# Linear-attention stage of a two-layer transformer: its loop over 128 units written out one to three units ahead

## The chip, the cores and the metric

One Trainium2 chip with 8 NeuronCores. All 8 cores run the same program, each on one sequence of 2048 tokens by 1024 features; they exchange nothing. The metric is the device time of the slowest core in microseconds (us), as the median of the timed runs.

## The reference, cut to what matters

The network has two pre-norm layers: ordinary attention and a ternary-weight feed-forward part in the first, linear attention and a gated feed-forward part in the second. The change touches only the linear attention of the second layer:

```python
def taylor_exp(x):                       # x: (b, h, l, 16) -> (b, h, l, 1 + 16 + 256)
    x2 = (x[..., :, None] * x[..., None, :]).reshape(*x.shape[:-1], d * d) / r2
    return jnp.concatenate([ones, x / rrd, x2 / rd], axis=-1)
q = (hidden @ Wq) ; k = (hidden @ Wk) ; v = (hidden @ Wv)     # 16 heads, q and k 16 wide, v 64 wide
qf, kf = taylor_exp(q), taylor_exp(k)
A = jnp.tril(jnp.einsum('bhnf,bhmf->bhnm', qf, kf))
y = jnp.einsum('bhnm,bhme->bhne', A, v)
z = 1.0 / (jnp.einsum('bhlf,bhlf->bhl', qf, jnp.cumsum(kf, axis=2)) + EPS)
out = (y * z[..., None]) ... @ Wo
```

## The kernel before

The program is a row of stages (`p0` to `p11`, all inside `build_program`). In each stage every engine has its own list of instructions, collected by a helper class `Ph` (its `op`, `wait` and `dma` record instructions, which is why nearly all of them carry line 52 in the profile, and waits line 84), and the stages are separated by a barrier. Engines are kept in step by hand: `ts` counts what TensorE has finished, `vs` what VectorE has, `ss` what ScalarE has, and `p.wait(engine, semaphore, value)` puts a wait into that engine's list. The order of each engine's work is exactly the order in which the Python code records it.

The changed stage is `p7` (from line 870 on). It computes the linear attention in chunks of 256 tokens. Its inputs lie in SBUF: `QF` and `KF` (projections with the feature on the partitions), `QTK` and `KTK` (the same with the token on the partitions, scaled) and `V1` (values, with a column of ones per head, so that the denominator is computed as a 65th output). A unit is one head and one chunk: `units` (line 905) has 16 heads by 8 chunks, 128 in all, with two heads (`lane` 0 and 1) alternating, so that unit `ui` and unit `ui - 2` belong to the same head and the state is carried from one to the other.

For each unit (loop at line 962) the code records, in this order:

1. VectorE: `RHQ` (the head's 16 rows of `QF`, by a mask), then the key features in `KFB`, per half chunk a product of 16 by 16 and a scaled copy, then a drain (lines 965 to 981).
2. ScalarE, from the second chunk on: the running state `PST` copied to `STSB` (lines 983 to 986).
3. TensorE: the score products `PG` (lines 988 to 998).
4. ScalarE: `ARAW`, the square of the shifted scores, since the second-order expansion of the exponential is a square plus 0.5 (line 1002).
5. VectorE: `ASB`, plus 0.5 and the triangular mask, three instructions (lines 1005 to 1012).
6. TensorE: `PY`, two products with the values, and from the second chunk on three with the state and the transposed query features `QFM`; then six products that add to the state `PST` (lines 1014 to 1045).
7. ScalarE: the reciprocal of the denominator as Ln, drain, Exp (`ZSC`, `Z`).
8. TensorE: `Z` broadcast over 64 partitions by a product with ones, written over `PG` (line 1054).
9. VectorE: `PY` copied to `YT`, a drain, and the product with the broadcast into `Y` (lines 1058 to 1067).
10. `prep_qf(ui + 2)` (line 950), if that unit isn't of chunk 0: VectorE builds the query features in `QFTK`, TensorE transposes them in two times three blocks to `PTR`, two tensors of 384 columns, and VectorE copies each to `QFM` (lines 927 to 942).

There are two buffers each of `KFB`, `QFTK`, `QFM`, `RHQ`, `ARAW`, `ASB`, `STSB`, `Z`, `YT`, and of the PSUM tensors `PST`, `PG`, `PY` and `PTR`, eight banks in all. The one transfer of the stage, the weights `WO1` of the next, is issued at its start.

Of the kernel before, what the change touches and what calls it, by code (L numbers as in the profile page):

```python
# [20 lines left out]
S1 = 1.0 / math.sqrt(4.0 * math.sqrt(2.0))  # L21
# [125 lines left out]
def build_program(T=2048, upto="p11", taps=()):  # L147
# [14 lines left out]
    nc = bass.Bass("TRN2", target_bir_lowering=False)  # L162
# [40 lines left out]
    dst = [Sem(st, nc, f"dst{i}") for i in range(2)]  # L203
# [7 lines left out]
    ts = Sem(st, nc, "ts")  # L211
# [128 lines left out]
    p = Ph()  # L340
# [529 lines left out]
    if act("p7"):  # L870
# [3 lines left out]
        with ExitStack() as ps:  # L874
            KFB = [ps.enter_context(nc.sbuf_tensor(f"KFB{i}", [128, 2 * 384], BF16)) for i in range(2)]
            QFTK = [ps.enter_context(nc.sbuf_tensor(f"QFTK{i}", [128, 2 * 384], BF16)) for i in range(2)]
            QFM = [ps.enter_context(nc.sbuf_tensor(f"QFM{i}", [128, 3 * 256], BF16)) for i in range(2)]
            RHQ = [ps.enter_context(nc.sbuf_tensor(f"RHQ{i}", [128, 256], BF16)) for i in range(2)]
# [8 lines left out]
            PY = [ps.enter_context(nc.psum_tensor(f"PY{i}", [65, 256], F32)) for i in range(2)]  # L887
            PTR = [ps.enter_context(nc.psum_tensor(f"PTR{i}", [128, 384], BF16)) for i in range(2)]
            zb_ts = {}

            p = Ph()
            p.dma("gpsimd", WO1[:, :], dram["wo1"], dq1)
            for b in KFB:
                p.add("vector", lambda v, b=b: v.memset(
                    b.rearrange("p (s f) -> p s f", s=2)[:, :, 0:1], 1.0))
                p.add("vector", lambda v, b=b: v.memset(
                    b.rearrange("p (s f) -> p s f", s=2)[:, :, 273:384], 0.0))
            for b in QFTK:
# [62 lines left out]

            for ui, (h, ch) in enumerate(units):
                lane = h // 8
                kc = lane
                p.wait("vector", ts, g_ts.get(ui - 2, 0))
                p.op("vector", "tensor_single_scalar", RHQ[lane][:, :],
                     QF[:, kc * T + ch * 256: kc * T + ch * 256 + 256],
                     HMASK[:, (h % 8):(h % 8) + 1], AL.mult)
                p.wait("vector", ts, state_ts.get(ui - 2, 0))
                for tsub in range(2):  # L970
                    tt = 2 * ch + tsub
                    src = KTK[:, tt * 256 + h * 16: tt * 256 + h * 16 + 16]
                    i0 = src.unsqueeze(1).broadcast_to([128, 16, 16])
                    i1 = src.unsqueeze(2).broadcast_to([128, 16, 16])
                    p.op("vector", "tensor_tensor",
                         KFB[lane][:, tsub * 384 + 17: tsub * 384 + 273].rearrange(
                             "p (i j) -> p i j", i=16), i0, i1, AL.mult)
                    p.op("vector", "tensor_scalar_mul",
                         KFB[lane][:, tsub * 384 + 1: tsub * 384 + 17], src, 0.5 / S1)
                p.op("vector", "drain", inc=vs)  # L980
                stage_vs = vs.n
                if ch > 0:
                    p.wait("scalar", ts, state_ts.get(ui - 2, 0))
                    p.wait("scalar", ts, y_ts.get(ui - 2, 0))
                    p.op("scalar", "activation", STSB[lane][:, :], PST[lane][:, :],
                         AF.Copy, inc=ss)
                    evac_ss[ui] = ss.n
                p.wait("tensor", vs, stage_vs)
                if ch > 0:
                    p.wait("tensor", ss, evac_ss[ui])  # L990
                p.wait("tensor", ss, araw_ss.get(ui - 2, 0))
                p.wait("tensor", vs, yv_vs.get(ui - 2, 0))
                p.op("tensor", "matmul", PG[lane][:, 0:256],
                     KF[:, kc * T + (2 * ch) * 128: kc * T + (2 * ch) * 128 + 128],
                     RHQ[lane][:, :], start=True, stop=True)
                p.op("tensor", "matmul", PG[lane][:, 256:384],
                     KF[:, kc * T + (2 * ch + 1) * 128: kc * T + (2 * ch + 1) * 128 + 128],
                     RHQ[lane][:, 128:256], start=True, stop=True, inc=ts)
                g_ts[ui] = ts.n
                p.wait("scalar", ts, g_ts[ui])  # L1000
                p.wait("scalar", vs, a_vs.get(ui - 2, 0))
                p.op("scalar", "activation", ARAW[lane][:, 0:384], PG[lane][:, 0:384],
                     AF.Square, scale=1.0 / math.sqrt(32.0), bias=CB[:, 2:3], inc=ss)
                araw_ss[ui] = ss.n
                p.wait("vector", ss, araw_ss[ui])
                p.wait("vector", ts, y_ts.get(ui - 2, 0))
                p.op("vector", "scalar_tensor_tensor", ASB[lane][:, 0:128],
# [4 lines left out]
                     ARAW[lane][:, 256:384], 0.5, TRIL[:, :], AL.add, AL.mult, inc=vs)  # L1012
                a_vs[ui] = vs.n
                p.wait("tensor", vs, a_vs[ui])
                p.wait("tensor", vs, yv_vs.get(ui - 2, 0))
                mms = [
# [17 lines left out]
                y_ts[ui] = ts.n  # L1034
                for tsub in range(2):
                    first = (ch == 0 and tsub == 0)
                    for fcx in range(3):
                        p.op("tensor", "matmul",
                             PST[lane][:, fcx * 65: fcx * 65 + 65],
                             KFB[lane][:, tsub * 384 + fcx * 128: tsub * 384 + fcx * 128 + 128],  # L1040
                             V1[:, (2 * ch + tsub) * 1040 + h * 65: (2 * ch + tsub) * 1040 + h * 65 + 65],
                             start=(first and fcx == 0), stop=(tsub == 1 and fcx == 2),
                             skip_group_check=True,
                             inc=(ts if (tsub == 1 and fcx == 2) else None))
                state_ts[ui] = ts.n
                p.wait("scalar", ts, y_ts[ui])
                p.wait("scalar", ts, zb_ts.get(ui - 2, 0))
# [4 lines left out]
                z1_ss = ss.n  # L1052
                p.wait("tensor", ss, z1_ss)
                p.op("tensor", "matmul", PG[lane][0:64, 0:256], ONES_B[64:65, 0:64],
                     Z1[lane][64:65, :], start=True, stop=True, skip_group_check=True,
                     inc=ts)
                zb_ts[ui] = ts.n
                p.wait("vector", ts, y_ts[ui])
                p.wait("vector", ss, z1_ss)
                p.wait("vector", vs, yv_vs.get(ui - 2, 0))  # L1060
# [4 lines left out]
                p.op("vector", "tensor_mul",
                     Y[64 * (h % 2): 64 * (h % 2) + 64,
                       (h // 2) * T + ch * 256: (h // 2) * T + ch * 256 + 256],
                     YT1[lane][:, :], PG[lane][0:64, 0:256], inc=vs)
                yv_vs[ui] = vs.n
                if ui + 2 < len(units):  # L1070
                    prep_qf(ui + 2)
            p.emit(nc)
# [174 lines left out]
```

How the kernel before makes its waits and increments, by code:

```python
        def f(e, meth=meth, a=a, kw=kw, tgt=tgt, inck=inck, lowp=lowp):  # L47
            if lowp:
                with e.bass.allow_low_precision("bf16 output by design"):
                    ins = getattr(e, meth)(*a, **kw)
            else:
                ins = getattr(e, meth)(*a, **kw)
            if tgt is not None:
                ins.then_inc(tgt, inck)
# [6 lines left out]
        def f(e, o=out_ap, i=in_ap, h=sem.h):  # L61
            e.dma_start(o, i).then_inc(h, 16)
# [6 lines left out]
        def f(e, o=out_ap, i=in_ap, h=sem.h):  # L69
            e.dma_start_transpose(o, i).then_inc(h, 16)
# [8 lines left out]
        def f(e, h=sem.h, v=v):  # L79
            e.wait_ge(h, v)
```

## Time and profile before

| | us |
|---|---|
| median of the timed runs | 4940.17 (4936.41 to 4943.93) |
| the profiled execution, whole | 4869.27 |
| its span, first to last instruction, slowest core | 4867.7 |
| spans of the 8 cores | 4851.3 to 4867.7 |
| granted TensorE clock, mean over the span, 1 is 2.4 GHz | 0.728 |

The table is to be read so: the timed runs have no profiler, and the profiled execution is a single one; durations of instructions come from it. Its time beside its span shows how little lies outside the recorded instructions.

### The profile page before, as it was taken

The numbers are of one execution on the slowest core, as the hardware profiler recorded it, in microseconds if no ns is written. First come the engines' busy times: TensorE is split into PE (matmuls) and PEld (weight loads), VectorE is DVE, ScalarE is ACT, GpSimd is POOL, SyncE is SP. The second block draws the span as 40 slices with busy tenths as digits, with TensorE's granted clock in tenths as the row PEclk, the third lists the DMA queues.
The fourth block names the chain that finished last, engine by engine and source line by source line (L and its number), as shares of the span: only waits on it lengthen the run. The fifth ranks groups of instructions, "written<-read, shape, count | busy, mean of one in ns | idle before, by whom it ended". The sixth has DMA issues, their size and how long they took to land. (4 is left out here: it accounts for less than half of the span.)

```text
span 4867.7 us, 39062 instructions; the slowest of 8 cores (4851.3 to 4867.7 us)
## 1 busy us (share of the span) xinstructions
PE 2552.6 (52%) x12011; PEld 1046.0 (21%) x12136; DVE 1620.0 (33%) x3557; ACT 1177.4 (24%) x1691; POOL 109.6 (2%) x162
## 2 busy tenths in 40 slices
PE   1556556456456500039996563333333336378877
PEld 0221111111112200014442331111111112133333
DVE  2332432432432464540002234444444443422221
ACT  1345245245245200023121211111111113211110
POOL 0000000000000001100000000000000000000000
PEclk8778678678678755569998775555555557699999
DMA  4000000000000075612321100000000000335525
GB/s 99 7 1 7 7 1 7 7 1 7 0 1 1 29 261 192 203 39 78 71 59 35 26 18 1 1 1 1 1 1 1 1 1 1 48 52 73 63 39 108
DMA packets 178933, 188.15 MB, mean 39 GB/s; under 512 B 118432, under 2 KB 159408, under 8 KB 175024
## 3 DMA queue, kind: packets, MB, share of 16 engines
q0 software_dynamic: 90400, 126.92, 12.5%
q1 hardware_dynamic: 88336, 58.72, 4.3%
q8 instruction: 108, 1.77, 0.2%
q14 instruction: 89, 0.73, 0.1%
HBM read 211.85 MB, written 25.17 MB: 49 GB/s over the span
## 5 line engine op out<-in xcount | busy, mean ns | idle before, releaser
L52 ACT ACTIVATE SCR<-S,NEGC 128x1024 bf16<-128x1024 f32 x512 | 548.2, 1112 | 151.5 <-PE S L52 147.7
L52 PE MATMUL PO<-SCR,VP 128*65 128x512 bf16 x1024 | 346.4, 423 | 168.5 <-ACT SCR L52 93.0
L52 DVE CAST Y<-PO 64x512 bf16<-64x512 f32 x64 | 43.7, 684 | 630.2 <-PE PO L52 629.7
L52 PE MATMUL PGU<-XLN,WGS 128*128 128x512 bf16 x752 | 181.1, 380 | 120.1 <-DVE HH L52 94.4
L52 DVE TENSOR_TENSOR X<-X,TF 128x512 f32<-128x512 f32 x64 | 44.3, 693 | 582.5 <-ACT TF L52 582.5
L52 PE MATMUL lnA<-lnXB,ONES_B 128*1 128x512 bf16 x128 | 56.9, 624 | 343.5 <-ACT lnXB L52 343.5
L52 ACT ACTIVATE ARAW<-PG,CB 128x384 bf16<-128x384 f32 x128 | 74.4, 581 | 665.3 <-PE PG L52 665.2
L52 PE MATMUL PH<-XLN,W1S 128*128 128x512 bf16 x1003 | 222.0, 381 | 17.2 <-DMA W1S<-w1b 15.1
L52 PE MATMUL PH<-HSB,W2S 128*128 128x512 bf16 x1004 | 220.3, 379 | 2.9 <-ACT HSB L52 1.9
L52 PE MATMUL S<-QP,KP 64*128 64x512 bf16 x1024 | 216.4, 430 | 5.1 <-DVE NEGC L52 5.1
L50 DVE RECIPROCAL DROW<-DROW 1x512 bf16<-1x512 bf16 x64 | 206.6, 3292 | 0.8
L52 PE MATMUL PG<-RHQ,KF 128*128 128x256 bf16 (+1 forms) x256 | 61.1, 341 | 269.4 <-DVEq L52 269.4
L52 PE MATMUL PTR<-IDN,QFTK 128*128 128x128 bf16 x672 | 89.5, 304 | 202.9 <-DVE QFTK L52 202.9
L52 PE MATMUL PAUX<-DROW,ONES_B 1*64 1x512 bf16 x64 | 38.4, 600 | 284.7 <-DVE DROW L50 232.4
L52 PE MATMUL PY<-ASB,V 128*65 128x256 bf16 (+1 forms) x256 | 64.1, 353 | 226.3 <-DVE ASB L52 226.3
L52 PE MATMUL PGU<-XLN,WUS 128*128 128x512 bf16 x753 | 180.6, 380 | 0.8
L52 ACT ACT_TABLE_LOAD x11 | 14.1, 1283 | 635.3 <-PEq L84 441.7
L52 PE MATMUL PGU<-HH,WDS 128*128 128x512 bf16 x752 | 165.4, 379 | 2.9 <-DVE HH L52 2.0
L52 DVE CAST YT<-PY 64x256 bf16<-64x256 f32 x128 | 53.4, 417 | 334.8 <-ACT Z L52 334.8
L52 DVE TENSOR_TENSOR TT<-SGT,PGU 128x512 bf16<-128x512 bf16 x96 | 66.0, 687 | 296.1 <-ACT SGT L52 296.1
L52 DVE SCALAR_TENSOR_TENSOR ASB<-ARAW,TRIL 128x128 bf16<-128x128 bf16 x256 | 73.8, 288 | 241.6 <-ACT ARAW L52 241.5
L52 ACT ACTIVATE SGT<-PGU 128x512 bf16<-128x512 f32 x96 | 57.3, 597 | 377.7 <-PE PGU L52 377.7
(157 smaller groups left out, 3708.8 us busy)
## 6 DMA issues: line engine op xcount, KB each, us to landing
WSL<-w POOLq DMA_DIRECT2D x16, 2048.0 KB, 11.8
WSL<-w POOLq DMA_DIRECT2D x64, 512.0 KB, 4.2
W1S<-w1b SPq DMA_DIRECT2D x16, 1024.0 KB, 5.4
W2S<-w2b SPq DMA_DIRECT2D x16, 1024.0 KB, 6.6
WGS<-wg POOLq DMA_DIRECT2D x12, 1024.0 KB, 9.2
WUS<-wu POOLq DMA_DIRECT2D x12, 1024.0 KB, 13.5
WDS<-wd POOLq DMA_DIRECT2D x16, 768.0 KB, 8.1
w1b<-WTB SPq DMA_DIRECT2D x8, 1024.0 KB, 5.0
```

Of the source, the lines that this page charges most:

```text
L50: ins = getattr(e, meth)(*a, **kw)
L52: ins = getattr(e, meth)(*a, **kw)
```

## The change

The loop body is cut into small functions, each recording one step of unit `i` on one engine, and a new loop calls them for different units. Buffers follow: `KFB` gets two per lane, `QFM` three, the two `PTR` become one of 768 columns, and the broadcast of `Z` gets a bank of its own, `PZB`, of which there is one.

```diff
-            KFB = [ps.enter_context(nc.sbuf_tensor(f"KFB{i}", [128, 2 * 384], BF16)) for i in range(2)]
+            KFB = [[ps.enter_context(nc.sbuf_tensor(f"KFB{i}_{j}", [128, 2 * 384], BF16))
+                    for j in range(2)] for i in range(2)]
-            QFM = [... for i in range(2)]
+            QFM = [... for i in range(3)]
-            PTR = [ps.enter_context(nc.psum_tensor(f"PTR{i}", [128, 384], BF16)) for i in range(2)]
+            PTR = ps.enter_context(nc.psum_tensor("PTR", [128, 768], BF16))
+            PZB = ps.enter_context(nc.psum_tensor("PZB7", [64, 256], F32))
...
+            def v_build(i):          # RHQ and KFB
+                p.wait("vector", ts, g_ts.get(i - 2, 0))
...
+                p.wait("vector", ts, state_ts.get(i - 4, 0))
...
+                p.op("vector", "drain", inc=vs)
+            def v_qft(i):            # QFTK
+                p.wait("vector", ts, tr_ts.get(i - 2, 0))
...
+            def t_tr(i):
+                p.wait("tensor", vs, qft_vs[i])
+                p.wait("tensor", vs, ptr_evac_vs.get(i - 2, 0))
...
+            def v_qfm_evac(i):
+                p.wait("vector", ts, tr_ts[i])
+                p.wait("vector", ts, y_ts.get(i - 3, 0))
+                src = PTR.rearrange("p (t c f) -> p t c f", t=2, c=3)
+                dst = QFM[i % 3].rearrange("p (c t f) -> p t c f", c=3, t=2)
+                p.op("vector", "tensor_copy", dst, src, inc=vs)
...
+            def t_g_state(i):        # PG, then the six products into PST
+                p.wait("tensor", vs, build_vs[i])
                 if ch > 0:
+                    p.wait("tensor", ss, evac_ss[i])
+                p.wait("tensor", ss, araw_ss.get(i - 2, 0))
...
+            def t_zb(i):
+                p.wait("tensor", ss, z_ss[i])
+                p.wait("tensor", vs, yv_vs.get(i - 1, 0))
+                p.op("tensor", "matmul", PZB[:, :], ONES_B[64:65, 0:64],
+                     Z1[lane][64:65, :], start=True, stop=True, inc=ts)
...
+            def v_yout(i):           # YT, drain, Y
...
+                p.wait("vector", ts, zb_ts[i])
+                p.op("vector", "tensor_mul", ..., YT1[lane][:, :], PZB[0:64, :], inc=vs)
...
+            v_build(0)
+            for j in (1, 2):
+                if j < NU:
+                    v_qft(j)
+
+            for i in range(NU):
+                t_g_state(i)
+                if i >= 1:
+                    t_zb(i - 1)
+                if i + 2 < NU:
+                    t_tr(i + 2)
+                if i + 1 < NU:
+                    s_evac(i + 1)
+                s_square(i)
+                v_poly(i)
+                if i + 2 < NU:
+                    v_qfm_evac(i + 2)
+                if i + 1 < NU:
+                    v_build(i + 1)
+                if i + 3 < NU:
+                    v_qft(i + 3)
+                t_y(i)
+                s_z(i)
+                if i >= 1:
+                    v_yout(i - 1)
+            t_zb(NU - 1)
+            v_yout(NU - 1)
```

TensorE's list for one unit in the middle of the stage, before the change; a name in brackets is the semaphore waited on (`vs` VectorE's, `ss` ScalarE's):

```order
L52 MATMUL PG<-RHQ,KF 128x256 [waits vs,ss]
L52 MATMUL PG<-RHQ,KF 128x128
L52 MATMUL PY<-ASB,V 65x256 [waits vs]
L52 MATMUL PY<-ASB,V 65x128
L52 MATMUL PY<-QFM,STSB 65x256 x3
L52 MATMUL PST<-V,KFB 128x65 x6
L52 MATMUL PG<-Z_1,ONES_B 64x256 [waits ss]
L52 MATMUL PTR<-IDN,QFTK 128x128 [waits vs]
L52 MATMUL PTR<-IDN,QFTK 128x128 x2
L52 MATMUL PTR<-IDN,QFTK 128x128 [waits vs]
L52 MATMUL PTR<-IDN,QFTK 128x128 x2
```

And the same place in the changed kernel:

```order
L52 MATMUL PG<-RHQ,KF 128x256 [waits vs,ss]
L52 MATMUL PG<-RHQ,KF 128x128
L52 MATMUL PST<-V,KFB_0 128x65 x6
L52 MATMUL PZB<-Z_1,ONES_B 64x256 [waits ss,vs]
L52 MATMUL PTR<-IDN,QFTK 128x128 [waits vs]
L52 MATMUL PTR<-IDN,QFTK 128x128 x5
L52 MATMUL PY<-ASB,V 65x256 [waits vs]
L52 MATMUL PY<-ASB,V 65x128
L52 MATMUL PY<-QFM,STSB 65x256 x3
```

The products into `PST` moved ahead of `PY`; the broadcast of `Z` (now that of the unit before) and the transposes (now of two units later) moved between them and `PY`, and the broadcast waits on VectorE too.

VectorE's list for one unit before the change, from the masks on:

```order
L52 SCALAR_TENSOR_TENSOR ASB<-ARAW,TRIL 128x128 [waits ss,ts]
L52 TENSOR_SCALAR ASB<-ARAW 128x128
L52 SCALAR_TENSOR_TENSOR ASB<-ARAW,TRIL 128x128
L52 CAST YT_1<-PY 64x256 [waits ts,ss,vs]
L52 TENSOR_TENSOR Y<-YT_1,PG 64x256 [waits ts]
L52 TENSOR_TENSOR QFTK<-QTK 128x256
...
L52 COPY QFM<-PTR 128x3x128 [waits ts] x2
L52 TENSOR_SCALAR RHQ<-QF,HMASK 128x256 [waits ts]
L52 TENSOR_TENSOR KFB<-KTK 128x256 [waits ts]
```

And in the changed kernel:

```order
L52 SCALAR_TENSOR_TENSOR ASB<-ARAW,TRIL 128x128 [waits ss,ts]
L52 TENSOR_SCALAR ASB<-ARAW 128x128
L52 SCALAR_TENSOR_TENSOR ASB<-ARAW,TRIL 128x128
L52 COPY QFM<-PTR 128x2x3x128 [waits ts]
L52 TENSOR_SCALAR RHQ<-QF,HMASK 128x256 [waits ts]
L52 TENSOR_TENSOR KFB_1<-KTK 128x256 [waits ts]
...
L52 TENSOR_TENSOR QFTK<-QTK 128x256 [waits ts]
...
L52 CAST YT_0<-PY 64x256 [waits ts,ss,vs]
L52 TENSOR_TENSOR Y<-YT_0,PZB 64x256 [waits ts]
```

`YT` and `Y` (of the unit before) moved from behind the masks to the end of the iteration, and one copy with a destination of one more dimension stands directly behind the masks.

## Rows read from the trace of the kernel before

**Rows 1.** The page's slices, 40 equal parts of the span, in tenths.

```profile
PE   1556556456456500039996563333333336378877
...
PEclk8778678678678755569998775555555557699999
```

**Rows 2.** Windows: length, busy PE, PEld, DVE, ACT, POOL, clock, DMA; timeline: last instruction.

```profile
2859.50:4059.00 1199.50, 406.71 (x2418) 213.06 (x2420) 490.56 (x1960) 214.05 (x497) 0.54 (x1) 0.50 0.01 2
...
4057.00 0.41 DVE L52 TENSOR_TENSOR Y<-YT,PG 64x256 bf16<-64x256 bf16 x1 [0.19 <-PE PG L52]
```

**Rows 3.** Waits in 2860 to 4058 us: waiter, releaser, total us, times, longest.

```profile
ACT ARAW L52 <- PE PG L52: 665.2, 127, 5.9
...
DVE YT L52 <- ACT Z L52: 334.8, 128, 3.0
...
PE PG L52 <- DVEq L52: 269.4, 128, 3.6
```

**Rows 4.** Timeline of one unit: start, duration, engine, instructions, idle before and releaser.

```profile
3397.09 0.48 PE L52 MATMUL PG<-RHQ,KF 128*128 128x256 bf16 x2 [2.05 <-DVEq L52]
3397.72 0.58 ACT L52 ACTIVATE ARAW<-PG,CB 128x384 bf16<-128x384 f32 x1 [5.60 <-PE PG L52]
3398.47 0.29 DVE L52 SCALAR_TENSOR_TENSOR ASB<-ARAW,TRIL 128x128 bf16<-128x128 bf16 x1 [1.88 <-ACT ARAW L52]
...
3398.78 0.28 DVE L52 SCALAR_TENSOR_TENSOR ASB<-ARAW,TRIL 128x128 bf16<-128x128 bf16 x1
...
3399.32 0.50 PE L52 MATMUL PY<-ASB,V 128*65 128x256 bf16 x2 [1.75 <-DVE ASB L52]
...
3400.75 0.38 ACT L52 ACTIVATE ZSC<-PY 1x256 f32<-1x256 f32 x1 [2.45 <-PE PY L52]
3401.19 0.41 ACT L52 ACTIVATE Z<-ZSC 1x256 bf16<-1x256 f32 x1
3401.62 0.34 ACT L52 ACTIVATE STSB<-PST 128x195 bf16<-128x195 f32 x1
...
3401.74 0.39 PE L52 MATMUL PG<-Z,ONES_B 1*64 1x256 bf16 x1 [0.71 <-ACT Z L52]
3401.77 0.42 DVE L52 CAST YT<-PY 64x256 bf16<-64x256 f32 x1 [2.71 <-ACT Z L52]
3402.38 0.41 DVE L52 TENSOR_TENSOR Y<-YT,PG 64x256 bf16<-64x256 bf16 x1 [0.19 <-PE PG L52]
3402.82 0.43 DVE L52 TENSOR_TENSOR QFTK<-QTK 128x256 bf16<-128x256 bf16 x1
...
3403.57 0.17 DVE L52 TENSOR_SCALAR QFTK<-QTK 128x16 bf16<-128x16 bf16 x1
...
3404.01 0.80 PE L52 MATMUL PTR<-IDN,QFTK 128*128 128x128 bf16 x6 [1.87 <-DVE QFTK L52]
3404.66 0.68 DVE L52 COPY QFM<-PTR 128x384 bf16<-128x384 bf16 x2 [0.91 <-PE PTR L52]
3405.25 0.28 DVE L52 TENSOR_SCALAR RHQ<-QF,HMASK 128x256 bf16<-128x256 bf16 x1
3405.45 0.42 DVE L52 TENSOR_TENSOR KFB<-KTK 128x256 bf16<-128x256 bf16 x1
...
3406.19 0.17 DVE L52 TENSOR_SCALAR KFB<-KTK 128x16 bf16<-128x16 bf16 x1
...
3406.86 0.48 PE L52 MATMUL PG<-RHQ,KF 128*128 128x256 bf16 x2 [2.05 <-DVEq L52]
```

**Rows 5.** The same unit by windows, columns as in rows 2.

```profile
3397.09:3406.86 9.77, 3.39 (x21) 1.77 (x22) 4.05 (x16) 1.70 (x4) 0.00 (x0) 0.50 0.00 0
```

**Rows 6.** Groups by line and form on VectorE, copies out of PSUM: count, busy us, mean ns.

```profile
L52 DVE COPY QFM<-PTR 128x384 bf16<-128x384 bf16 x224 | 75.9, 358 | 103.8 <-PE PTR L52 102.9 <-issue 1.0
L52 DVE CAST YT<-PY 64x256 bf16<-64x256 f32 x128 | 53.4, 417 | 334.8 <-ACT Z L52 334.8
...
L52 DVE CAST Y<-PO 64x512 bf16<-64x512 f32 x64 | 43.7, 684 | 630.2 <-PE PO L52 629.7
```

More of the change, by code:

```diff
@@ L874, in build_program @@
         with ExitStack() as ps:
-            KFB = [ps.enter_context(nc.sbuf_tensor(f"KFB{i}", [128, 2 * 384], BF16)) for i in range(2)]
+            KFB = [[ps.enter_context(nc.sbuf_tensor(f"KFB{i}_{j}", [128, 2 * 384], BF16))
+                    for j in range(2)] for i in range(2)]
             QFTK = [ps.enter_context(nc.sbuf_tensor(f"QFTK{i}", [128, 2 * 384], BF16)) for i in range(2)]
-            QFM = [ps.enter_context(nc.sbuf_tensor(f"QFM{i}", [128, 3 * 256], BF16)) for i in range(2)]
+            QFM = [ps.enter_context(nc.sbuf_tensor(f"QFM{i}", [128, 3 * 256], BF16)) for i in range(3)]
             RHQ = [ps.enter_context(nc.sbuf_tensor(f"RHQ{i}", [128, 256], BF16)) for i in range(2)]
@@ L887, in build_program @@
             PY = [ps.enter_context(nc.psum_tensor(f"PY{i}", [65, 256], F32)) for i in range(2)]
-            PTR = [ps.enter_context(nc.psum_tensor(f"PTR{i}", [128, 384], BF16)) for i in range(2)]
-            zb_ts = {}
+            PTR = ps.enter_context(nc.psum_tensor("PTR", [128, 768], BF16))
+            PZB = ps.enter_context(nc.psum_tensor("PZB7", [64, 256], F32))
             p = Ph()
             p.dma("gpsimd", WO1[:, :], dram["wo1"], dq1)
[L893 to L897, printed above, removed]
+            for bb in KFB:
+                for b in bb:
+                    p.add("vector", lambda v, b=b: v.memset(
+                        b.rearrange("p (s f) -> p s f", s=2)[:, :, 0:1], 1.0))
+                    p.add("vector", lambda v, b=b: v.memset(
+                        b.rearrange("p (s f) -> p s f", s=2)[:, :, 273:384], 0.0))
             for b in QFTK:
@@ L960, in build_program, with U @@
                 prep_qf(1)
-            for ui, (h, ch) in enumerate(units):
+            def U(i):
+                return units[i]
+            def v_build(i):
+                h, ch = U(i)
                 lane = h // 8
-                kc = lane
-                p.wait("vector", ts, g_ts.get(ui - 2, 0))
+                kb = (i // 2) % 2
+                p.wait("vector", ts, g_ts.get(i - 2, 0))
                 p.op("vector", "tensor_single_scalar", RHQ[lane][:, :],
-                     QF[:, kc * T + ch * 256: kc * T + ch * 256 + 256],
+                     QF[:, lane * T + ch * 256: lane * T + ch * 256 + 256],
                      HMASK[:, (h % 8):(h % 8) + 1], AL.mult)
-                p.wait("vector", ts, state_ts.get(ui - 2, 0))
+                p.wait("vector", ts, state_ts.get(i - 4, 0))
                 for tsub in range(2):
@@ L980, in build_program @@
                 p.op("vector", "drain", inc=vs)
-                stage_vs = vs.n
-                if ch > 0:
[L983 to L990, printed above, removed]
@@ L991, in build_program @@
-                p.wait("tensor", ss, araw_ss.get(ui - 2, 0))
-                p.wait("tensor", vs, yv_vs.get(ui - 2, 0))
+                build_vs[i] = vs.n
+            def v_qft(i):
+                h, ch = U(i)
+                if ch == 0:
+                    return
+                buf = i % 2
+                p.wait("vector", ts, tr_ts.get(i - 2, 0))
+                for tsub in range(2):
+                    tt = 2 * ch + tsub
+                    src = QTK[:, tt * 256 + h * 16: tt * 256 + h * 16 + 16]
+                    i0 = src.unsqueeze(1).broadcast_to([128, 16, 16])
+                    i1 = src.unsqueeze(2).broadcast_to([128, 16, 16])
+                    p.op("vector", "tensor_tensor",
+                         QFTK[buf][:, tsub * 384 + 17: tsub * 384 + 273].rearrange(
+                             "p (i j) -> p i j", i=16), i0, i1, AL.mult)
+                    p.op("vector", "tensor_scalar_mul",
+                         QFTK[buf][:, tsub * 384 + 1: tsub * 384 + 17], src, 0.5 / S1,
+                         inc=(vs if tsub == 1 else None))
+                qft_vs[i] = vs.n
@@ new lines, in t_tr @@
+            def t_tr(i):
+                h, ch = U(i)
+                if ch == 0:
+                    tr_ts[i] = ts.n
+                    return
+                p.wait("tensor", vs, qft_vs[i])
+                p.wait("tensor", vs, ptr_evac_vs.get(i - 2, 0))
+                for tsub in range(2):
+                    for fcx in range(3):
+                        p.op("tensor", "transpose",
+                             PTR[:, tsub * 384 + fcx * 128: tsub * 384 + fcx * 128 + 128],
+                             QFTK[i % 2][:, tsub * 384 + fcx * 128: tsub * 384 + fcx * 128 + 128],
+                             IDN[:, :],
+                             inc=(ts if (tsub, fcx) == (1, 2) else None))
+                tr_ts[i] = ts.n
@@ new lines, in v_qfm_evac, with s_evac @@
+            def v_qfm_evac(i):
+                h, ch = U(i)
+                if ch == 0:
+                    return
+                p.wait("vector", ts, tr_ts[i])
[3 more added lines that the diff above has]
+                p.op("vector", "tensor_copy", dst, src, inc=vs)
+                ptr_evac_vs[i] = vs.n
+            def s_evac(i):
+                h, ch = U(i)
+                lane = h // 8
+                if ch == 0:
+                    return
+                p.wait("scalar", ts, state_ts.get(i - 2, 0))
+                p.wait("scalar", ts, y_ts.get(i - 2, 0))
+                p.op("scalar", "activation", STSB[lane][:, :], PST[lane][:, :],
+                     AF.Copy, inc=ss)
+                evac_ss[i] = ss.n
@@ new lines, in t_g_state @@
+                for tsub in range(2):
+                    first = (ch == 0 and tsub == 0)
+                    for fcx in range(3):
+                        p.op("tensor", "matmul",
+                             PST[lane][:, fcx * 65: fcx * 65 + 65],
+                             KFB[lane][kb][:, tsub * 384 + fcx * 128: tsub * 384 + fcx * 128 + 128],
+                             V1[:, (2 * ch + tsub) * 1040 + h * 65: (2 * ch + tsub) * 1040 + h * 65 + 65],
+                             start=(first and fcx == 0), stop=(tsub == 1 and fcx == 2),
+                             skip_group_check=True,
+                             inc=(ts if (tsub == 1 and fcx == 2) else None))
@@ L1002, in build_program, with s_square @@
+                state_ts[i] = ts.n
+            def s_square(i):
+                h, ch = U(i)
+                lane = h // 8
+                p.wait("scalar", ts, g_ts[i])
+                p.wait("scalar", vs, a_vs.get(i - 2, 0))
                 p.op("scalar", "activation", ARAW[lane][:, 0:384], PG[lane][:, 0:384],
                      AF.Square, scale=1.0 / math.sqrt(32.0), bias=CB[:, 2:3], inc=ss)
-                araw_ss[ui] = ss.n
-                p.wait("vector", ss, araw_ss[ui])
-                p.wait("vector", ts, y_ts.get(ui - 2, 0))
+                araw_ss[i] = ss.n
@@ L1007, in build_program, with v_poly @@
+            def v_poly(i):
+                h, ch = U(i)
+                lane = h // 8
+                p.wait("vector", ss, araw_ss[i])
+                p.wait("vector", ts, y_ts.get(i - 2, 0))
                 p.op("vector", "scalar_tensor_tensor", ASB[lane][:, 0:128],
@@ L1012, in build_program, with t_y @@
                      ARAW[lane][:, 256:384], 0.5, TRIL[:, :], AL.add, AL.mult, inc=vs)
-                a_vs[ui] = vs.n
-                p.wait("tensor", vs, a_vs[ui])
-                p.wait("tensor", vs, yv_vs.get(ui - 2, 0))
+                a_vs[i] = vs.n
+            def t_y(i):
+                h, ch = U(i)
+                lane = h // 8
+                p.wait("tensor", vs, a_vs[i])
+                p.wait("tensor", vs, yv_vs.get(i - 2, 0))
                 mms = [
@@ L1033, in build_program, with s_z @@
                          inc=(ts if mi == len(mms) - 1 else None))
[L1034 to L1047, printed above, removed]
+                y_ts[i] = ts.n
+            def s_z(i):
+                h, ch = U(i)
+                lane = h // 8
+                p.wait("scalar", ts, y_ts[i])
+                p.wait("scalar", ts, zb_ts.get(i - 2, 0))
                 p.op("scalar", "activation", ZSC1[lane][64:65, :], PY[lane][64:65, :], AF.Ln)
@@ L1051, in build_program @@
                      AF.Exp, scale=-1.0, inc=ss)
[L1052 to L1060, printed above, removed]
+                z_ss[i] = ss.n
+            def t_zb(i):
+                h, ch = U(i)
+                lane = h // 8
+                p.wait("tensor", ss, z_ss[i])
+                p.wait("tensor", vs, yv_vs.get(i - 1, 0))
+                p.op("tensor", "matmul", PZB[:, :], ONES_B[64:65, 0:64],
+                     Z1[lane][64:65, :], start=True, stop=True, inc=ts)
+                zb_ts[i] = ts.n
+            def v_yout(i):
+                h, ch = U(i)
+                lane = h // 8
+                p.wait("vector", ts, y_ts[i])
+                p.wait("vector", ss, z_ss[i])
+                p.wait("vector", vs, yv_vs.get(i - 2, 0))
                 p.op("vector", "tensor_copy", YT1[lane][:, :], PY[lane][0:64, :])
-                p.op("vector", "drain", inc=vs)
-                yt_vs[ui] = vs.n
-                p.wait("vector", ts, zb_ts[ui])
+                p.op("vector", "drain")
+                p.wait("vector", ts, zb_ts[i])
                 p.op("vector", "tensor_mul",
@@ L1067, in build_program @@
                        (h // 2) * T + ch * 256: (h // 2) * T + ch * 256 + 256],
[L1068 to L1071, printed above, removed]
+                     YT1[lane][:, :], PZB[0:64, :], inc=vs)
+                yv_vs[i] = vs.n
+            g_ts = {}; araw_ss = {}; a_vs = {}; y_ts = {}
+            yv_vs = {}; state_ts = {}; evac_ss = {}
+            build_vs = {}; qft_vs = {}; tr_ts = {}; ptr_evac_vs = {}
+            zb_ts = {}; z_ss = {}
+            NU = len(units)
+            v_build(0)
[24 more added lines that the diff above has]
+            v_yout(NU - 1)
             p.emit(nc)
```

21 lines of the change are left out of this document (11 added, 10 removed).

## The prediction

> **What bounds the kernel now.** I read the page's slices first, then the stretch that the diff touches, then its waits, then one unit of it in order of time. In the slices [rows 1] the stage is the long plain in the middle: TensorE at 3 tenths (slices 25 to 33) and the clock at 5. The stage runs from its memsets at 2859.5, where the window starts, to the end of the last normalised `Y` at 4057.00 + 0.41 us, 1197.9 us, a quarter of the span; in the window TensorE is busy 407 us, VectorE 491 and ScalarE 214 of 1199.5, with next to no DMA, at a granted clock of 0.50, which is the 1.2 GHz level [rows 2]. No engine is full, so it is bound by a chain of hand-overs. The longest waits say the same [rows 3]: ScalarE before `ARAW` for `PG`, VectorE before `YT` for `Z`, TensorE before `PG` for VectorE's queue, 128 times each: every engine idles for a result of the unit in hand. That ScalarE's is the largest (665 us) is no loss by itself, since it has little to do.
>
> One unit in order of time [rows 4] shows the chain closing on itself. From `PG` at 3397.09 to the next `PG` at 3406.86 is 9.77 us, and nothing overlaps: score product, square, mask and add, five `PY` products, Ln and Exp, broadcast `Z`, copy `YT`, product `Y`, build `QFTK`, transposes, copy `QFM`, build `RHQ` and `KFB`, next `PG`. VectorE works 4.05 us of those 9.77 and TensorE 3.39 [rows 5]. The 128 units have 16 with chunk 0, which skip the query features; the other 112 at 9.76 us make 1093 us, and the rest of the stage gives about 6.5 us to each of the 16.
>
> **What the change does, part by part.** The loop is written out in another order. The numbers of products, builds and ScalarE operations stay; 224 copies of 384 columns from `PTR` become 112 of 768; four small memsets are added. The query features are built three units ahead, transposed two ahead, the key features one ahead, and the broadcast of `Z` and the final product come one unit late. So the chain of a unit no longer closes in one unit. What remains are three rings, priced start to start from [rows 4].
>
> First VectorE alone, since it has the most work: the masks, 3398.47 to 3398.78 + 0.28, 0.59 long, and since the next instruction starts some 0.08 before the end of the last (`RHQ` at 3405.25, the copies until 3405.34) 0.51 to the next start; the copy of `PTR`, taken below as 0.48; `RHQ` to `KFB` 0.20; `KFB` 0.91 (3405.45 to 3406.19 + 0.17) and about 0.16 for the drain and the wait behind it (`YT` ends at 3402.19, `Y` starts at 3402.38, 0.19 with a drain and a wait in between), 1.07; `QFTK` 0.82 to where the next may start (3402.82 to 3403.57 + 0.17, less the 0.1 by which instructions overlap); `YT` with its drain 0.60; `Y` 0.45. Sum 4.13 us; with what the waits on two semaphores add before the masks I take 4.2 to 4.3.
>
> The copy of 768 columns isn't in this trace. The nearest rows [rows 6]: 384 bf16 columns from PSUM take 358 ns, 256 f32 columns 417 ns and 512 f32 columns 684 ns. The last two give 1.04 ns a column and 0.15 us fixed; with the same 0.15 the copy of 384 runs at 0.54 ns a column. So 768 take 0.15 + 768 x 0.54 = 0.57 us if the fast rate holds, 0.15 + 768 x 1.04 = 0.95 if the more broken destination loses it. I take 0.57, whose next instruction starts at 0.48: it is the nearer row, the same data type and source. The other end adds 0.38 us a unit.
> The Trainium skill ("VectorE: DVE Perf Modes", What auto-detection actually checks) ties the fast rate to 16-bit elements at unit step, which both copies have; by it the low end stands. No run here has shown it.
>
> Second, a ring that the new order makes. `PZB` is single, so the broadcast of unit i-1 on TensorE waits for the product `Y` of unit i-2 (`yv_vs.get(i - 1, 0)` in `t_zb`), which is the last thing VectorE does in an iteration. TensorE is in order: the six transposes stand behind that broadcast, and VectorE needs them for its copy, second in its next iteration. The ring: on VectorE copy 0.48, `RHQ` 0.20, `KFB` 1.07, `QFTK` 0.82, `YT` 0.60, `Y` 0.41, together 3.58. Then to TensorE 0.14 (`Z` ends 3401.60, `PG` starts 3401.74). Then broadcast to first transpose 0.24: 256 columns at 1.2 GHz are 0.21, and two waits stand there. Then the transposes 0.80 and 0.17 to VectorE past two waits (`ARAW` ends 3398.30, `ASB` starts 3398.47). Sum 3.58 + 0.14 + 0.24 + 0.97 = 4.93 us. The masks (0.5 us) fit into the wait for the transposes, so they add nothing. This ring is longer than VectorE's work by about 0.65 us and sets the unit.
>
> Third, the ring through ScalarE: `PY` to `ZSC` 1.43 (3399.32 to 3400.75), to `STSB` 0.87, then `ARAW` about 0.40 later (it now stands behind `STSB`), to `ASB` 0.75, to `PY` 0.85: 4.30 us, under 4.93. The state products now stand before `PY` and no longer delay it.
>
> A unit with chunk 0 has no copy and no build of `QFTK` in the ring: 4.93 - 0.48 - 0.82 = 3.63 us. The stage becomes 112 x 4.93 + 16 x 3.63 = 610 us, plus 2 us of start and added memsets: 612. It saves 1197.9 - 612 = 586 us. The other stages touch none of this: `WO1` lands during the stage either way. The profiled execution took 4869.3 us, of which 4867.7 are the span, so it would take 4283. The timed runs of the kernel before have their median at 4940, 70.9 us (1.5%) above the profiled one; the trace doesn't say where. Kept as a constant it gives 4354, kept as a ratio 4346; I take 4352.
>
> What hides the rest: TensorE has 3.4 us of work in 4.93, so products at half clock are covered except the broadcast and the transposes, which lie on the ring. If the cover of the masks is lost (VectorE late for another reason) 0.5 us a unit returns, 60 us. Extra wait instructions cost about 0.1 us each on TensorE (one wait: 0.14 from `Z` to `PG`; two: 3399.06 to 3399.32 from `ASB` to `PY`, 0.26), and there are no more of them than before.
>
> **The rivals.**
> A, the broadcast doesn't delay. If `Y` of the iteration before is done early, or VectorE lags, the unit is VectorE's own work, 4.27 us. With 16 x 2.97 for chunk 0 and the 2 us the stage is 528 us and the time 4268. For it: 4.13 is only 0.8 below the ring. Against it: the program order puts the transposes behind the broadcast, and `Y` last on VectorE.
>
> B, the copy at the slow rate: 4.93 + 0.38 = 5.31 us in 112 units, 43 us more, 4395. For it: the destination has one more dimension. Against: rate of the row for 384, whose destination is already broken in three.
>
> C, the clock. TensorE's busy share rises from 3.39 of 9.77 to 3.39 of 4.93. In the slices with TensorE at 5 to 6 tenths (4 in two of them; slices 2 to 14) the granted clock is 6 to 8 tenths [rows 1], against 5 here. At 2.4 GHz the five starts between the transposes go from 0.107 to 0.053 each, 0.27 us off the ring; the two waits keep the broadcast where it is. 4.66 us, 30 us less, 4322. Against: those slices mix dense stretches with idle ones, while here the work stays broken up.
> The Trainium skill ("TensorE: Matmul & The Clock Gate", What's actually happening) says that the low level is the default and that activity lifts it, which speaks for C; a later part of the page, on PE-mode transposes, says they do not count as activity in the same way, which speaks against. No row here shows a stage of this density.
>
> D, slower than before. If the rings closed in one unit after all (place: the wait of `t_zb` and the in-order queue behind it), the chain would be `RHQ` and `KFB` 1.11, drain and four waits 0.50, `PG` to `ARAW` 0.63, to `ASB` 0.75, to `PY` 0.85, to `ZSC` 1.43, to end of `Z` 0.85, to the broadcast 0.14, transposes 0.24 + 0.97, copy 0.48 and then `QFTK`, `YT` and `Y` 1.83, 9.78 us, the 9.77 of before; with two doubled hand-overs (0.25) it is 10.03, 30 us slower, 4970. It would decide from 9.77 us a unit; for over 2% it takes 10.7. Against it: the broadcast concerns the unit before, and in the code the ring from copy to copy by way of `PG`, masks, `PY` and `Z` spans two units: the first eleven of those terms, 7.95, over two, 3.98 us.
>
> That the change doesn't do what it says: the orders show it done on both engines, so only a hidden wait could undo it, which is D.
>
> **How the numbers follow.** Forecast (ring of `PZB`, 4.93) 0.66; A 0.14; B 0.10; C 0.09; D 0.01. The range takes A and B in and 30 us beyond B for waits that I undercount: 4265 to 4425. A measurement of this kernel tells about 2% from no change, and all cases but D are some 10% faster: faster 0.98, within 2% 0.01, slower 0.01.
>
> **What would show it.** Right: a stage of about 612 us with a unit of 4.9; VectorE's idle time nearly all before the copy `QFM`, waiting for `PTR`, about 0.6 to 0.7 us a unit; TensorE's before the broadcast, waiting for VectorE's `Y`; the copy at about 0.57 us; clock still 0.50. A would show no wait before `QFM` and the unit at 4.3; B the copy at 0.95; C a clock above 0.5 in the stage. I am wrong in kind if the unit is over 6 us or if ScalarE's hand-over stands last before the masks.

## The result and the profile after

The changed kernel has a median of 4345.9 us (4298.85 to 4428.23, 11 runs); the kernel before, on the same chip, 4908.4 us (4872.02 to 4963.15, 10 runs). The ratio is 0.8823, with a 95% interval of 0.877 to 0.8876: 11.8% less time. The ratio, here and in the experiments, leaves out the executions in which the cores of one die ran at a lower granted clock, while the medians hold them, so that the two medians do not divide to it. Forecast were 4352 us in a range of 4265 to 4425, against the 4940 of the runs shown before.

The page of the profiled execution, its first line and the slices:

```profile
span 4298.1 us, 38629 instructions; the slowest of 8 cores (4276.8 to 4298.1 us)
...
PE   1456565655656455000179995585555582779777
...
DVE  2432324233241434545510003157777754231231
...
PEclk8687777867777687555589997785555576999999
```

Against [rows 1] the long plain of nine slices has become one of five (28 to 32, with a slice at either end that the stage fills in part): TensorE at 5 tenths instead of 3, VectorE at 7 instead of 4, and the clock still at 5. The span is 569.6 us shorter (4867.7 less 4298.1).

The stage by windows, from its first memset to the end of the last `Y` (length; busy us and count of PE, PEld, DVE, ACT, POOL; clock; DMA):

```profile
2857.80:3487.10 629.30, 368.30 (x2416) 232.29 (x2416) 465.56 (x1852) 214.15 (x497) 0.53 (x1) 0.50 0.02 4
```

The stage takes 629 us where [rows 2] had 1197.9: 569 us less, which is the span's gain but for 1 us, so the other stages gave and took next to nothing. Busy time moved little beside that (VectorE 466 for 491, TensorE 368 for 407, ScalarE 214 for 214), so it is mainly the idle time that went, and the granted clock is 0.50, the 1.2 GHz level, as before.

The longest waits in the stage (waiter, releaser, total us, times, longest):

```profile
ACT ZSC L52 <- PE PY L52: 351.8, 128, 3.3
...
PE PZB L52 <- DVE Y L52: 100.2, 111, 1.4
DVE QFM L52 <- PE PTR L52: 97.2, 111, 1.3
...
PE PG L52 <- ACT Z L52: 94.9, 90, 1.1
```

VectorE's wait of [rows 3], 334.8 us for `Z`, is gone; what is left on it is one wait of 0.87 us a unit for the transposes. TensorE's largest is for `Y`. These two lines are the ring that the prediction named. (The last line is not a second one: in the code `PG` has no wait for the `Z` that the row names. It waits for the builds, whose drain on VectorE ends just before.) One turn of it, from copy to copy, in the timeline:

```profile
3225.65 0.56 DVE L52 COPY QFM<-PTR 128x768 bf16<-128x768 bf16 x1 [0.95 <-PE PTR L52]
3226.13 0.28 DVE L52 TENSOR_SCALAR RHQ<-QF,HMASK 128x256 bf16<-128x256 bf16 x1
3226.32 0.42 DVE L52 TENSOR_TENSOR KFB<-KTK 128x256 bf16<-128x256 bf16 x1
...
3227.42 0.43 DVE L52 TENSOR_TENSOR QFTK<-QTK 128x256 bf16<-128x256 bf16 x1 [0.19 <-issue]
...
3228.25 0.41 DVE L52 CAST YT<-PY 64x256 bf16<-64x256 f32 x1
3228.25 0.58 ACT L52 ACTIVATE ARAW<-PG,CB 128x384 bf16<-128x384 f32 x1 [0.31 <-PE PG L52]
3228.80 0.41 DVE L52 TENSOR_TENSOR Y<-YT,PZB 64x256 bf16<-64x256 bf16 x1
3229.14 0.28 DVE L52 SCALAR_TENSOR_TENSOR ASB<-ARAW,TRIL 128x128 bf16<-128x128 bf16 x1
...
3229.36 0.39 PE L52 MATMUL PZB<-Z,ONES_B 1*64 1x256 bf16 x1 [0.93 <-DVE Y L52]
3229.45 0.28 DVE L52 SCALAR_TENSOR_TENSOR ASB<-ARAW,TRIL 128x128 bf16<-128x128 bf16 x1
3229.68 0.82 PE L52 MATMUL PTR<-IDN,QFTK 128*128 128x128 bf16 x6
...
3230.68 0.56 DVE L52 COPY QFM<-PTR 128x768 bf16<-128x768 bf16 x1 [0.95 <-PE PTR L52]
```

It reads: copy to `RHQ` 0.48, to `KFB` 0.19, to `QFTK` 1.10, to `YT` 0.83, to `Y` 0.55, its duration 0.41, to the broadcast `PZB` 0.15, to the first transpose 0.32, the six 0.82, to the copy 0.18; together 5.03 us for a unit that took 9.77 [rows 4]. The masks end at 3229.73 and then VectorE stands still for 0.95 us, although its next instructions, `RHQ` and `KFB`, need nothing from the transposes. `ARAW` is not late: the masks start as soon as VectorE has done `Y`.

### The profile page after: what moved, and what is told of

Read it like the earlier page. It is cut to its first block and busy times, and to the rows that moved or that the text cites. A ratio compares the mean times of both kernels' runs of the same rounds, so it can differ in the third digit from the quotient of the medians.

```text
span 4298.1 us, 38629 instructions; the slowest of 8 cores (4276.8 to 4298.1 us)
## 1 busy us (share of the span) xinstructions
PE 2521.5 (59%) x12136; PEld 1065.3 (25%) x12136; DVE 1594.9 (37%) x3449; ACT 1177.1 (27%) x1691; POOL 110.5 (3%) x162
## 5 line engine op out<-in xcount | busy, mean ns | idle before, releaser
L52 PEld LDWEIGHTS PO<-SCR,VP 128*65 128x65 bf16 x1024 | 76.6, 115 | 333.2 <-issue 333.2
L52 PE MATMUL PAUX<-SCR,NRM 128*1 128x512 bf16 x128 | 73.0, 570 | 136.0 <-DVE NRED L52 111.8
L52 ACT ACTIVATE ZSC<-PY 1x256 f32<-1x256 f32 x128 | 48.1, 376 | 351.8 <-PE PY L52 351.8
L52 PEld LDWEIGHTS PH<-XLN,W1S 128*128 128x128 bf16 x1024 | 100.4, 98 | 139.9 <-issue 20.4
```

The costliest lines, as they stand in the source:

```text
L52: ins = getattr(e, meth)(*a, **kw)
```

## The experiments

Eight kernels were run, in two groups of four (the changed kernel unedited is one of them, in the second group); each ratio is to the kernel before in the same group, and where the stage is given it is that of the profiled execution's slowest core (memsets to the last `Y`), the unit the median distance of two products `Y`. Where a stage is said to be so much over or under the changed kernel, its 628 to 629 us are meant.

**The transposes ahead of the broadcast.** In the loop:

```diff
                 t_g_state(i)
-                if i >= 1:
-                    t_zb(i - 1)
                 if i + 2 < NU:
                     t_tr(i + 2)
+                if i >= 1:
+                    t_zb(i - 1)
```

> Edit: the changed kernel with the six transposes recorded ahead of the broadcast of Z. Theory (the ring of the single PZB, copy to copy, 5.03 us a unit, because the transposes stand behind a broadcast that waits for VectorE's last product): the wait before the copy QFM goes, the unit falls to 4.27 us, set by the ring through ScalarE (PY, ZSC, Z, STSB, ARAW, ASB), the stage from 629 to about 547 us, the profiled execution from 4300 to about 4217. Rival (the wait before QFM only shifts, VectorE's own work with its semaphore instructions is the bound at nearly 5 us): unit 4.9 to 5.0, gain under 15 us.

Measured: median 4219.03 us, ratio 0.8641 (0.8568 to 0.8714), profiled span 4216.4, stage 545 us, unit 4.27. A stretch of its timeline:

```profile
3215.61 0.80 PE L52 MATMUL PTR<-IDN,QFTK 128*128 128x128 bf16 x6 [0.16 <-issue]
3215.67 0.58 ACT L52 ACTIVATE ARAW<-PG,CB 128x384 bf16<-128x384 f32 x1
3215.82 0.42 DVE L52 TENSOR_TENSOR Y<-YT,PZB 64x256 bf16<-64x256 bf16 x1 [0.15 <-issue]
3216.38 0.39 PE L52 MATMUL PZB<-Z,ONES_B 1*64 1x256 bf16 x1
3216.42 0.29 DVE L52 SCALAR_TENSOR_TENSOR ASB<-ARAW,TRIL 128x128 bf16<-128x128 bf16 x1 [0.19 <-PE PTR L52]
```

The transposes now start before `Y`, the broadcast is behind them, and there is 0.19 us before the masks where there was 0.95 before the copy. (The row puts the 0.19 down to `PTR`, but the masks wait for `ARAW`, which ends at 3216.25, 0.17 before them.) No instruction was added or taken away, two calls changed places, and 84 us of stage went (629 to 545). The ring through `PZB` did set the unit; the rival, that VectorE's work alone was the bound at 5 us, is out.

**The square ahead of the state's copy, on top of that.** On ScalarE:

```diff
+                s_square(i)
                 if i + 1 < NU:
                     s_evac(i + 1)
-                s_square(i)
```

> Edit: e1 (transposes ahead of the broadcast) and the square ARAW of unit i ahead of the copy STSB of unit i+1 on ScalarE. Theory (in e1 the ring PY, ZSC, Z, STSB, ARAW, ASB sets the 4.27 us, so taking STSB's 0.34 us out of it shows): unit 3.95 us, then VectorE's own work, stage about 515, 30 us under e1, 112 under the changed kernel. Rival (e1's 4.27 is already VectorE's own work, which the prediction put at 4.2 to 4.3): unit 4.27, as e1 within 5 us.

Measured: median 4197.89, ratio 0.8613 (0.8596 to 0.863), span 4195.0, stage 523 us, unit 4.10. The direction is the theory's, the size is 22 us of stage and not 30. In its timeline VectorE goes nearly without a wait:

```profile
3209.16 0.41 DVE L52 TENSOR_TENSOR Y<-YT,PZB 64x256 bf16<-64x256 bf16 x1
...
3209.61 0.29 DVE L52 SCALAR_TENSOR_TENSOR ASB<-ARAW,TRIL 128x128 bf16<-128x128 bf16 x1
...
3210.12 0.55 DVE L52 COPY QFM<-PTR 128x768 bf16<-128x768 bf16 x1
...
3210.59 0.27 DVE L52 TENSOR_SCALAR RHQ<-QF,HMASK 128x256 bf16<-128x256 bf16 x1
...
3210.78 0.42 DVE L52 TENSOR_TENSOR KFB<-KTK 128x256 bf16<-128x256 bf16 x1
...
3211.88 0.43 DVE L52 TENSOR_TENSOR QFTK<-QTK 128x256 bf16<-128x256 bf16 x1 [0.19 <-PE PY L52]
...
3212.71 0.41 DVE L52 CAST YT<-PY 64x256 bf16<-64x256 f32 x1
```

The only gap left there is 0.19 us behind the drain of `KFB` (the row names `PY`, for which `QFTK` has no wait in the code). From `Y` to the masks are 0.45 us (3209.16 to 3209.61). That is a unit of a head with an odd number; in the heads with an even number they are 0.33 to 0.34:

```profile
3156.91 0.41 DVE L52 TENSOR_TENSOR Y<-YT,PZB 64x256 bf16<-64x256 bf16 x1
3157.24 0.28 DVE L52 SCALAR_TENSOR_TENSOR ASB<-ARAW,TRIL 128x128 bf16<-128x128 bf16 x1
```

`Y` itself takes 0.41 us in both. So this kernel has two units, 3.98 us in the even heads and 4.10 in the odd ones, and the median of 4.10 stands for the second alone. 3.98 is the 3.95 of this expectation, whose `Y` to the masks was 0.34; 4.10 is the sum that the prediction made (4.13), whose `Y` of 0.45 came from an odd head. The 0.12 us in every other block of 16 units make most of the 8 us by which the stage is longer than expected. The kernel before shows the same two distances behind `Y`, 0.34 and 0.45, in the same heads. In the code an even head's `Y` is written to partitions 0 to 63, where its operands lie, and an odd head's to 64 to 127; behind an odd head's `Y` the masks start 0.03 to 0.04 us after its end, behind an even head's 0.07 before it. Whether the partitions are the reason was not tried. This is the fastest version that was run, 13.9% under the kernel before.

**The same edit alone.**

> Edit: the changed kernel with only the square ARAW ahead of STSB on ScalarE. Theory (the ring of PZB alone sets the unit): no change, within 5 us of the changed kernel, unit 5.03. Rival (ScalarE's ring and the ring of PZB both contribute): 10 to 40 us less.

Measured: ratio 0.8827 (0.8806 to 0.8848), unit 5.03, stage 628 us, on core 5 as on the slowest core. Nothing: with the ring of `PZB` in front, taking 0.34 us off ScalarE's ring is worth nothing, and behind it 22 us. The two rings do not add up, the longer one counts.

**The changed kernel again, on this chip.**

> The changed kernel itself, unedited, on the same chip as the other three. Unit 5.03 us, stage 629, profiled execution about 4300 us, ratio to the kernel before 0.877 to 0.888.

Measured: ratio 0.883 (0.8812 to 0.8847), span 4304.2, stage 628, unit 5.03.

**`YT` and `Y` right behind the masks.**

```diff
                 v_poly(i)
+                if i >= 1:
+                    v_yout(i - 1)
                 if i + 2 < NU:
                     v_qfm_evac(i + 2)
...
                 s_z(i)
-                if i >= 1:
-                    v_yout(i - 1)
```

> Edit: the changed kernel with YT and Y of unit i-1 directly behind the masks of unit i on VectorE, ahead of the copy QFM, the builds and QFTK; TensorE's order stays. Theory: PZB comes free 2.6 us earlier in the iteration, so the broadcast and the transposes no longer wait for VectorE, but the broadcast of a unit now has to be done before VectorE can go on, and RHQ and KFB end later: a new ring through ScalarE and the builds, unit about 4.8 us, stage about 610, 15 to 25 us less than the changed kernel. Rival (only the wait for PZB counts): unit 4.27, 80 us less.

Measured: ratio 0.8806 (0.8785 to 0.8828), stage 615 us, 13 under the changed kernel and so a little less than the 15 to 25 expected; the unit is 4.75 us in even heads and 4.87 in odd ones, 4.78 as the median. Here `PZB` is free early and TensorE doesn't wait for `Y` any more, yet the gain is a sixth of that of the first experiment. The timeline shows the new ring:

```profile
3211.84 0.48 PE L52 MATMUL PG<-RHQ,KF 128*128 128x256 bf16 x2 [1.42 <-ACT STSB L52]
...
3212.47 0.58 ACT L52 ACTIVATE ARAW<-PG,CB 128x384 bf16<-128x384 f32 x1 [0.68 <-PE PG L52]
...
3213.22 0.29 DVE L52 SCALAR_TENSOR_TENSOR ASB<-ARAW,TRIL 128x128 bf16<-128x128 bf16 x1 [0.66 <-ACT ARAW L52]
...
3213.74 0.41 DVE L52 CAST YT<-PY 64x256 bf16<-64x256 f32 x1
...
3214.30 0.41 DVE L52 TENSOR_TENSOR Y<-YT,PZB 64x256 bf16<-64x256 bf16 x1 [0.15 <-issue]
...
3214.64 0.54 DVE L52 COPY QFM<-PTR 128x768 bf16<-128x768 bf16 x1
3215.10 0.27 DVE L52 TENSOR_SCALAR RHQ<-QF,HMASK 128x256 bf16<-128x256 bf16 x1
...
3216.59 0.48 PE L52 MATMUL PG<-RHQ,KF 128*128 128x256 bf16 x2 [1.25 <-ACT Z L52]
```

`PG`, `ARAW` 0.63 later, masks 0.75, `YT` 0.52, `Y` 0.56, copy 0.34, `RHQ` 0.46, and 1.49 from there through `KFB`, its drain and the waits to the next `PG`: 4.75. VectorE waits 0.66 us before the masks, and the 0.9 us of `YT` and `Y` now stand ahead of the builds, on which the next `PG` depends. A wait can be cured at either end; which one is better is decided by what that moves onto the other rings: here exchanging two calls on TensorE gave 84 us and moving `YT` and `Y` on VectorE 13.

**Undoing the parts.** Three kernels give up one kind of lateness or lead each; the rest of the change stays.

The broadcast and the product in their own iteration again:

```diff
-                if i >= 1:
-                    t_zb(i - 1)
...
                 s_z(i)
-                if i >= 1:
-                    v_yout(i - 1)
-            t_zb(NU - 1)
-            v_yout(NU - 1)
+                t_zb(i)
+                v_yout(i)
```

> Edit: the changed kernel, but the broadcast of Z and the product Y of a unit are in the unit's own iteration again, as before the change; the key and query features stay ahead. Theory: there was already a ring of 5.03 us, so giving up the lateness costs little: unit about 5.1 to 5.2, stage 640 to 655, +15 to +25 us over the changed kernel. Rival (running Y one unit late is what broke the chain, so without it the chain closes in one unit again): unit above 7 us, over 200 us slower than the changed kernel.

Measured: ratio 0.8877 (0.8811 to 0.8943), unit 5.10, stage 650, 21 us over the changed kernel's.

`RHQ` and `KFB` not ahead:

```diff
-            v_build(0)
...
             for i in range(NU):
+                v_build(i)
                 t_g_state(i)
...
-                if i + 1 < NU:
-                    v_build(i + 1)
```

> Edit: the changed kernel with RHQ and KFB built in the unit's own iteration, at its start, not one ahead. Theory (rings): the score products wait for builds that stand behind VectorE's last product, unit about 5.6 us, stage about 710, +75 to +85 us over the changed kernel. Rival (the bound is VectorE's amount of work, whose sum is the same): no change within 15 us.

Measured: ratio 0.9015 (0.8939 to 0.9091), unit 5.76, stage 728, 99 us over, so more than the 75 to 85 expected. Its waits, and a piece of its timeline:

```profile
PE PG L52 <- DVEq L52: 276.8, 121, 4.9
DVE ASB L52 <- ACT ARAW L52: 227.5, 128, 2.7
```

```profile
3229.00 0.82 PE L52 MATMUL PTR<-IDN,QFTK 128*128 128x128 bf16 x6
3229.30 0.29 DVE L52 SCALAR_TENSOR_TENSOR ASB<-ARAW,TRIL 128x128 bf16<-128x128 bf16 x1 [1.66 <-ACT ARAW L52]
...
3230.00 0.56 DVE L52 COPY QFM<-PTR 128x768 bf16<-128x768 bf16 x1
```

TensorE stands before `PG` for the builds, and VectorE before the masks for the square of that `PG`. The copy starts 0.70 us after the first mask and not 0.51, 0.18 after the end of the transposes at 3229.82: they are a little late here too, and the 0.19 us cover the 0.16 by which the unit is over the expected 5.6.

The query features at the end of the iteration, as before:

```diff
-            for j in (1, 2):
-                if j < NU:
-                    v_qft(j)
+            v_qft(1)
+            t_tr(1)
+            v_qfm_evac(1)
...
-                if i + 2 < NU:
-                    t_tr(i + 2)
...
-                if i + 2 < NU:
-                    v_qfm_evac(i + 2)
...
-                if i + 3 < NU:
-                    v_qft(i + 3)
...
                 if i >= 1:
                     v_yout(i - 1)
+                if i + 2 < NU:
+                    v_qft(i + 2)
+                    t_tr(i + 2)
+                    v_qfm_evac(i + 2)
```

> Edit: the changed kernel with QFTK, the transposes and the copy of unit i+2 at the end of the iteration i as in the kernel before, one after the other; the rest stays. Theory (rings): VectorE waits for the transposes with nothing else to do, and they stand behind the broadcast: unit about 6.0 us, stage about 745, +110 to +125 us over the changed kernel. Rival (the query features are only a filler and cost nothing wherever they stand): within 20 us.

Measured: ratio 0.9097 (0.9022 to 0.9172), unit 6.05, stage 753, 125 us over. Its waits:

```profile
PE PTR L52 <- DVE QFTK L52: 229.0, 111, 2.9
ACT ARAW L52 <- PE PG L52: 213.9, 109, 2.8
```

TensorE stands before the transposes for `QFTK`, 2.1 us each of 111 times, and in its list the next unit's `PG` comes behind them, for which ScalarE waits in turn.

In all three the theory's unit came within 0.2 us (5.1 to 5.2, 5.6 and 6.0 expected), and the rivals are out: the first would have had a unit above 7 us, the others no loss beyond 15 and 20 us. What follows: undone alone, each lead costs 99 and 125 us of stage, and the lateness of the broadcast and product, which looks like the core of the change, only 21 us, since the place that it was given made a ring of 5.03 us. What that lateness is worth with the transposes in front, where the unit is 4.27 us, was not run. Their sum is 245 of 569 us: undone alone, none brings the chain of before back, since the other leads still let the units overlap. How they would add up when undone in pairs was not tried.

## Why the prediction was right

*What bounds the kernel before.* Right as far as it went: the idle time went and the work stayed. That no engine was full is shown by the result.

*VectorE's own work, 4.13 us.* Right for odd heads, 0.15 too long for even ones: 4.10 and 3.98 are the units of the kernel with both edits, whose VectorE in the main waits for nothing but the drain. The 0.1 to 0.2 us that the prediction put on top for waits before the masks (4.2 to 4.3) do not show there. With the ring longer and VectorE's work shorter than taken, VectorE's wait before the copy is 0.87 us a unit and not the 0.6 to 0.7 foretold.

*The copy of 768 columns, 0.57 us.* Right. The group after is

```profile
L52 DVE COPY QFM<-PTR x112: 551/558/558, 2863.7 to 3475.4; 128x768 bf16<-128x768 bf16 x112
```

(min, median, max in ns), 558 for 2 x 384 columns where [rows 6] has 358 for 384: 200 ns more for 384 more columns, 0.52 a column. Rival B is out. The rule of the Trainium skill ("VectorE: DVE Perf Modes", What auto-detection actually checks) that ties the fast rate to 16-bit elements at unit step held for a destination of one more dimension.

*The ring of `PZB`, 4.93 us.* Right in place and kind, short by 0.10. The term that was mis-sized is "broadcast to first transpose 0.24": it is 0.32. The rest came out as put down within 0.05 each: on VectorE 3.56 for 3.58, 0.15 for 0.14, 0.82 + 0.18 for 0.97. The 0.24 took the 0.21 of the 256 columns and left 0.03 for the two waits that stand between, though the prediction itself puts a wait on TensorE at about 0.1; in the rows the first transpose starts 0.32 us behind the broadcast, 0.11 more than the columns. That the waits make the difference was not tried. Over 112 units 0.10 makes 11 of the 17 us by which the stage is longer than forecast (629 for 612); seven units of about 5.4 us and eight of 5.09 instead of 5.03 give some 3 more.

*The ring through ScalarE, 4.30 us, under the other.* Right, and shown: with the transposes in front the unit is 4.27, and its timeline has this ring term by term:

```profile
3221.71 0.50 PE L52 MATMUL PY<-ASB,V 128*65 128x256 bf16 x2 [0.67 <-DVE ASB L52]
...
3223.13 0.38 ACT L52 ACTIVATE ZSC<-PY 1x256 f32<-1x256 f32 x1 [2.44 <-PE PY L52]
...
3224.01 0.34 ACT L52 ACTIVATE STSB<-PST 128x195 bf16<-128x195 f32 x1
...
3224.38 0.58 ACT L52 ACTIVATE ARAW<-PG,CB 128x384 bf16<-128x384 f32 x1
...
3225.13 0.29 DVE L52 SCALAR_TENSOR_TENSOR ASB<-ARAW,TRIL 128x128 bf16<-128x128 bf16 x1 [0.19 <-PE PTR L52]
...
3225.98 0.50 PE L52 MATMUL PY<-ASB,V 128*65 128x256 bf16 x2 [0.51 <-DVE ASB L52]
```

That is 1.42 for 1.43, 0.88 for 0.87, 0.37 for 0.40, 0.75 and 0.85 as put down, together 4.27. Taking `STSB` out of that ring shortens the unit, while with the ring of `PZB` in place the same edit does nothing.

*Chunk 0 at 3.63 us.* Fits: the stage less 112 x 5.03 is 66 us; less about 3 us of start and the 3 of the longer units it is 60, about 3.75 each for 16.

*The sum.* 586 us were forecast to go and 569 went, 3% less. From the profiled executions it is 4300 against the 4283 forecast. That the median is right within 6 us is partly luck: it is 46 us over the profiled execution, where 69 were carried over, from two runs that are the eighth and ninth of ten by length (4872 to 4963 us). These 23 us too many make up for the 17 by which the stage was forecast too short.

*The rivals.* A was not the case: its sign would have been no wait before `QFM`, and there is one of 0.87 us. Its unit of 4.27 us turns up when two calls change places (545 us of stage; A said 528), but there the ring through ScalarE sets it. VectorE's own work sets the unit only in the kernel with both edits, and there it is 3.98 and 4.10. C, the clock: 0.50 in the stage with TensorE at 368 of 629 us busy, so it didn't rise; nor did it in the kernel with both edits, 0.50 at 389 of 523:

```profile
2861.50:3384.19 522.69, 389.25 (x2416) 226.60 (x2416) 455.38 (x1852) 201.76 (x497) 0.54 (x1) 0.50 0.03 5
```

Of the two statements of the Trainium skill ("TensorE: Matmul & The Clock Gate") the one that PE-mode transposes do not count as activity in the same way (Part 4) points this way, but no run separates it from the small idle times that both kernels still have. D, the ring that closes in one unit, is out by the unit of 5.03.

## What to carry to other kernels

After software pipelining, list the rings that are left, from an instruction to the same one of the next unit, across engines and with the queue order as a link of its own, and price each start to start from the trace before: the longest is the new unit. The three rings here came out within 0.15 us. Count every wait that stands in a queue on the ring: the term with two of them in it was the largest error of the longest ring. Look in the longest ring for an instruction that waits only because it stands behind another in an in-order queue (here six transposes behind a broadcast whose single buffer was busy): exchanging two calls was worth 84 us, nearly as much as a whole lead. Shortening a ring that wasn't the longest gave nothing here until the longest was cut, so try such edits in combination too.

## What was unexpected

The lateness of the broadcast and the final product, which needs a bank of its own, is worth 21 of 569 us as placed. The granted clock stayed at 0.50 with TensorE busy for 74% of the stage (389 of 523 us). And units are very regular (5.03) but for seven of 5.4 us: in three of them the copy `QFM` starts 0.53 to 0.54 us behind the last transpose and not 0.18, in the other four `Y` starts 0.91 us behind `YT` and not 0.56. They are not chance: within either kind most lie 52 units apart, and the repetition of the changed kernel has them at the same seven units. Nothing in the views says what VectorE waited for there.
